# Attention with two heads per stack on the two row halves of TensorE, scores in a ring of three banks

## What is computed

```python
mod = silu(c) @ w_adaln + b_adaln                  # six shifts, scales and gates
h = modulate(ln(x), sh_msa, sc_msa)
q, k, v = heads(h @ w_qkv + b_qkv)                 # 16 heads, 18 channels each
attn = softmax(einsum('bhqd,bhkd->bhqk', q, k) * hd ** -0.5)
x = x + g_msa * (merge(einsum('bhqk,bhkd->bhqd', attn, v)) @ w_proj + b_proj)
xn = modulate(ln(x), sh_mlp, sc_mlp)
# top 2 of 4 experts: cw * (gelu(xn @ w1 + b1) @ w2 + b2), summed
return x + g_mlp * moe
```

## Time and profile before

| | |
|---|---|
| median of 3 runs | 991.68 us (991.67 to 992.36) |
| the profiled execution, its own time | 992.99 us |
| its span, first to last instruction | 991.2 us |
| TensorE busy | 900.9 us (91%), 5111 matmuls |
| TensorE weight loads | 639.9 us (65%) |
| VectorE, ScalarE, GpSimd busy | 566.0, 516.8, 313.3 us |
| DMA | 73.99 MB, mean 75 GB/s |
| scores and maxima on TensorE | 486 + 512 matmuls recorded, 212.4 and 167.7 us busy |
| exponentials on ScalarE, maxima on VectorE | 282.0 and 309.2 us |

### The profile page before, as it was taken

One profiled execution on the slowest core, in us unless ns is written; L12 is line 12 of the kernel. 1 busy time (PEld: TensorE's weight loads), 2 busy tenths in 40 slices (PEclk: granted clock), 3 DMA queues, 4 the chain that ended last, 5 costly groups with the idle time before them and its releaser, 6 DMA issues. The chain is left out here.

```text
span 991.2 us, 15201 instructions
## 1 busy us (share of the span) xinstructions
PE 900.9 (91%) x5111; PEld 639.9 (65%) x5111; DVE 566.0 (57%) x978; ACT 516.8 (52%) x1003; POOL 313.3 (32%) x314
## 2 busy tenths in 40 slices
PE   4878799999999999999999896438999999999995
PEld 3775444454545545555444375328999999999995
DVE  3767658767676776767774068463455444444342
ACT  1531266777776777777778735435443333333331
POOL 3522111012120111111042149626555444444342
PEclk9898799999999999999999969558999999999998
DMA  8051600624216060330631157405332222222221
GB/s 209 10 114 23 129 3 17 131 84 102 64 27 137 17 128 19 74 84 8 153 98 44 35 162 256 149 25 141 84 60 56 44 43 43 36 41 40 43 36 19
DMA packets 59296, 73.99 MB, mean 75 GB/s; under 512 B 24856, under 2 KB 51334, under 8 KB 58200
## 3 DMA queue, kind: packets, MB, share of 16 engines
q1 hardware_dynamic: 50216, 60.32, 24.5%
q0 software_dynamic: 8400, 12.12, 7.3%
q10 hardware_dynamic: 608, 0.59, 0.2%
HBM read 33.87 MB, written 15.73 MB: 50 GB/s over the span
## 5 line engine op out<-in xcount | busy, mean ns | idle before, releaser
L1014 DVE TENSOR_REDUCE negmax<-m_ps 128x1 f32<-128x1024 f32 x256 | 309.2, 1221 | 129.5 <-PE m_ps L1079 128.8
L1001 ACT ACTIVATE probs<-s_ps 128x512 f32<-128x512 f32 x486 | 282.0, 597 | 102.6 <-PE s_ps L1110 79.8
L1110 PE MATMUL s_ps<-stack 96*128 96x512 f32 x486 | 212.4, 444 | 5.4 <-ACT probs L1001 3.6
L1110 PEld LDWEIGHTS s_ps<-stack 96*128 96x128 f32 x486 | 90.7, 189 | 163.0 <-ACT probs L1001 130.3
L1079 PE MATMUL m_ps<-stack 96*128 96x512 f32 x512 | 167.7, 412 | 13.1 <-DVE negmax L1014 7.4
L449 POOL TENSOR_TENSOR parts<-proj_f,parts 128x512 fp32r<-128x512 f32 x32 | 41.0, 1282 | 322.0 <-ACT proj_f L443 322.0
L1124 PE MATMUL o_ps<-probs,v_aug 128*19 128x512 f32 x1024 | 136.1, 604 | 0.5 <-ACT probs L1001 0.5
L1969 PE MATMUL gate_bank<-weights,ht_hi 128*128 x630 | 127.1, 296 | 0.4 <-DVE ht_lo L1865 0.4
L1079 PEld LDWEIGHTS m_ps<-stack 96*128 96x128 f32 x512 | 97.9, 195 | 35.2 <-DVE negmax L1014 16.7
L1945 PE MATMUL h_ps<-weights,xt_hi 128*128 x525 | 115.7, 351 | 4.1 <-DVE xt_hi L1858 4.1
L1691 ACT CAST ht_hi<-ht_ps 128x384 fp32r<-128x384 f32 x105 | 43.5, 488 | 117.4 <-PE ht_ps L1956 117.4
(11 more groups left out here) (213 smaller groups left out, 1111.7 us busy)
## 6 DMA issues: line engine op xcount, KB each, us to landing
stack<-parts SPq DMA_DIRECT2D x96, 256.0 KB, 5.0
w_raw<-in_L_cond_w SPq DMA_DIRECT2D x9, 432.0 KB, 3.6
w_raw<-in_L_cond_w SPq DMA_DIRECT2D x9, 384.0 KB, 3.4
xn_scratch<-h SPq DMA_DIRECT2D x16, 192.0 KB, 3.7
x_in<-in_x SPq DMA_DIRECT2D x4, 576.0 KB, 9.6
o_scratch<-o_norm SPq DMA_DIRECT2D x16, 144.0 KB, 2.4
o_in<-o_scratch SPq DMA_DIRECT2D x16, 144.0 KB, 2.6
xr<-in_x SPq DMA_DIRECT2D x16, 144.0 KB, 3.1
```

The lines of the kernel that those rows point to most:

```text
L1001: nc.scalar.activation(probs[:, st % 2, h], score_bank(g, st, h), ACT.Exp, scale=SCALE)\
L1014: nc.vector.tensor_reduce(negmax[:, half, g % 2, m % 16:m % 16 + 1], m_ps[m % 2][:], AX.X, ALU.max, negate=True).then_inc(max_free, 1)
L1110: nc.tensor.matmul(score_bank(g, st, h), stack[s][:, h, 1, kt // QT, (kt % QT) * P:(kt % QT + 1) * P], stack[s][:, h, 0, half], start=True ...
```

## The change

- A stack now has 128 rows: two heads, each in a block of 64 rows (54 used for the three products of 18 rows, and two rows for the high and low part of the maximum; ones stand against these, written once by memsets on GpSimd). There are three stack buffers (`STACKS = 3`), and the stack of group g+2 is loaded in group g, by 12 transfers of 18 rows each.
- The maxima are matmuls of one head, 128 queries and 512 keys; a pair of two heads fills the two halves of a double bank, and one reduction gives two numbers. A second small reduction joins the two key halves. Scores are issued in pairs.
- `misc` is gone. Scores and projection units share a ring of three single banks (`s_ps`, `slot_mm`, `slot_free`), and rows and outputs take turns in the maxima's two double banks (`max_mm`, `max_free`). `MaxPlan` makes the list of turns: maxima run 12 steps ahead, rows are due at steps 4 and 12, outputs at 2 and 10; projection units stand at steps 2, 5, 9 and 12, each cut in two.
- ScalarE takes a projection out once; GpSimd makes the high part by a copy, and the low part.
- The last group no longer uses four banks.
- SyncE's loop has another order, and a row of maxima goes back by four transfers of one row instead of two.

The diff, cut to its core:

```diff
+    BLOCK = 64
+    MAX_ROW = 3 * HD
+    STACKS = 3
...
+    def ones_rows(self, pool, i):
+
+        for hh in range(2):
+            s = slice(hh * self.BLOCK + HP, (hh + 1) * self.BLOCK)
+            pool.memset(f32(self.stacks[i][s, :, 1]), 1.0).then_inc(self.ones_ok, 1)
+            pool.wait_ge(self.ones_ok, 2 * i + hh + 1)
...
-        sp.wait_ge(self.parts_ok, 4 * (g + 1))
-
-        n = HP
+        sp.wait_ge(self.parts_ok, self.parts_count(g, 3))
+        sp.wait_ge(self.ones_ok, 2 * min(g + 1, self.STACKS))
...
-                sp.dma_start(f32(self.stacks[g % 2][q * HP:q * HP + n, h]).rearrange("p a b n -> p a (b n)"),
-                             f32(self.parts[h * HP:h * HP + n, kind]).rearrange("p a b n -> p a (b n)"))\
+                row = (h % 2) * self.BLOCK + q * HD
+                sp.dma_start(f32(self.stacks[g % self.STACKS][row:row + HD, h // 2]).rearrange("p a b n -> p a (b n)"),
+                             f32(self.parts[h * HP:h * HP + HD, kind]).rearrange("p a b n -> p a (b n)"))\
...
+PAIR_BLOCKS = 2
+S_BANKS = 3
+AHEAD = 48
+RATE = 4
+PROJ_AT = (2, 5, 9, 12)
+UNITS = len(PROJ_AT)
+
+
+def score_item(g, st, h):
+
+    before = sum(GH * STEPS + UNITS * (i + 2 < GG) for i in range(g))
+    return UNITS + before + GH * st + h + sum(st > at for at in PROJ_AT if g + 2 < GG)
...
+        self.maxima(self.lead, BLOCKS)
+        self.turn(self.lead, "rows", 0)
+        self.maxima(self.lead, AHEAD)
+        due = []
+        for t, items in enumerate(self.steps):
+            g, st = t // STEPS, t % STEPS
+            begun = self.block // BLOCKS
+            self.maxima(items, AHEAD + RATE * t + 2)
+            for turn in due:
+                self.turn(items, "rows", turn)
+            if st == KT + 2:
+                self.turn(items, "out", 2 * g)
+            if st == 2 and g >= 1:
+                self.turn(items, "out", 2 * g - 1)
+            self.maxima(items, AHEAD + RATE * (t + 1))
+            due = range(begun, self.block // BLOCKS)
...
-                n, s = 2 * g + half, g % 2
-                sp.wait_ge(rows_step, 2 * (n + 1))
+                sp.wait_ge(max_free, 2 + plan.rows_at[2 * g + half] + 1)
                 for part, rows in enumerate((rows_hi, rows_lo)):
-                    sp.dma_start(rows_dram[g, half, part], f32(rows[:, half])).then_inc(rows_st[half], 16)
+                    sp.dma_start(rows_dram[g, half, part].rearrange("a b n -> (a b) n"), f32(rows[:, half]))\
+                      .then_inc(rows_st[half], 16)
                 sp.wait_ge(rows_st[half], 32 * (g + 1))
-                for part, q in enumerate((0, 2)):
-                    sp.dma_start(f32(stack[s][q * HP + HD:q * HP + HA, :, 0, half]),
-                                 rows_dram[g, half, part].rearrange("(a h t) n -> a h (t n)", a=1, h=GH))\
-                      .then_inc(rows_ld[half], 16)
+                for part in range(2):
+                    for hh in range(2):
+                        row = hh * heads.BLOCK + heads.MAX_ROW + part
+                        sp.dma_start(f32(stack[g % heads.STACKS][row:row + 1, :, 0, half]),
+                                     rows_dram[g, half, part, hh].rearrange("(a j t) n -> a j (t n)", a=1, j=PAIRS))\
+                          .then_inc(rows_ld[half], 16)
...
             load_rows_of_max(0, 0)
+            load_stack(1)
             for g in range(GG):
-                if g + 1 < GG:
-                    load_stack(g + 1)
-                if g == 0:
-                    load_rows_of_max(0, 1)
-                else:
-                    load_rows_of_max(g, 1)
+                load_w(g + 3)
+                if g >= 1:
                     store(g - 1, 1)
+                load_rows_of_max(g, 1)
+                if g + 2 < GG:
+                    load_stack(g + 2)
...
+                store(g, 0)
                 if g + 1 < GG:
                     load_rows_of_max(g + 1, 0)
-                store(g, 0)
                 if g == GG - 2:
                     for i in (2, 3):
                         late.load_piece(sp, 0, i)
-                load_w(g + 3)
...
+            def parts(g, u):
+                half, a = u // 2, u % 2
+                hi, lo = ((heads.Q_HI, heads.Q_LO), (heads.K_HI, heads.K_LO))[a]
+                pool.wait_ge(slot_free, S_BANKS + proj_item(g, u) + 1)
+                if u == 0:
+                    for h in range(GH):
+                        pool.wait_ge(stack_ld[h], 48 * g)
+                nc.gpsimd.tensor_copy(heads.parts[:, hi, half], heads.proj_f[:, u % 2]).then_inc(parts_ok, 1)
+                pool.wait_ge(parts_ok, heads.parts_count(g, u) - 1)
+                nc.gpsimd.tensor_tensor(heads.parts[:, lo, half], heads.proj_f[:, u % 2],
+                                        f32(heads.parts[:, hi, half]), ALU.subtract).then_inc(parts_ok, 1)
...
+                    if st == 0 and g >= 1:
+                        out_of_bank(2 * g - 1)
+                    if st == KT:
+                        out_of_bank(2 * g)
+                    if st in PROJ_AT and g + 2 < GG:
+                        project(g + 2, PROJ_AT.index(st))
...
+                nc.vector.tensor_reduce(negmax[:, half, first:first + count], m_ps[n % 2][:], AX.X, ALU.max, negate=True)\
+                  .then_inc(max_free, 1)
+                if first + count == BLOCKS:
+                    dve.wait_ge(max_free, 2 + n + 1)
+                    nc.vector.tensor_reduce(rowmax[:, half].rearrange("p (h b) -> p b h", h=2),
+                                            negmax[:, half].rearrange("p (b k h) -> p b h k", k=2, h=2), AX.X, ALU.min)\
+                      .then_inc(rowmax_ok, 1)
...
+                for i in range(count):
+                    if half == 0 and (first + i) % (BLOCKS // PAIRS) == 0:
+                        for hh in range(2):
+                            pe.wait_ge(stack_ld[2 * ((first + i) // (BLOCKS // PAIRS)) + hh], 48 * (g + 1))
+                    hh, kh, qt, j = ((first + i) % 2, (first + i) // 2 % 2, (first + i) // 4 % QT,
+                                     (first + i) // (4 * QT))
+                    r = slice(hh * heads.BLOCK, hh * heads.BLOCK + heads.MAX_ROW)
+                    mm = nc.tensor.matmul(m_ps[n % 2][:, i], stack[s][r, j, 0, half, qt * P:(qt + 1) * P], stack[s][r, j, 1, kh],
                                           start=True, stop=True)
...
+                for hh in range(2):
+                    k = score_item(g, st, 2 * j + hh)
+                    pe.wait_ge(slot_free, k + 1)
+                    r = slice(hh * heads.BLOCK, hh * heads.BLOCK + heads.MAX_ROW + 2)
+                    nc.tensor.matmul(s_ps[k % S_BANKS][:], stack[s][r, j, 1, kt // QT, (kt % QT) * P:(kt % QT + 1) * P],
+                                     stack[s][r, j, 0, half], start=True, stop=True).then_inc(slot_mm, 1)
...
+                for st in range(STEPS):
+                    items = plan.steps[STEPS * g + st]
+                    scores(g, st, 0)
+                    for it in items[:1]:
+                        item(*it)
                     if st >= 1:
                         values(g, st - 1)
                     elif g >= 1:
                         values(g - 1, STEPS - 1)
-                    scores(g, st, (2,))
-                    for tile in tiles[1:2]:
-                        maximum(*tile)
-                    scores(g, st, (3,))
-                    for tile in tiles[2:]:
-                        maximum(*tile)
-                    for turn in row_turns:
-                        rows(*turn)
-                    for turn in out_turns:
-                        outputs(*turn)
-                    for unit in units:
-                        project(*unit)
+                    scores(g, st, 1)
+                    for it in items[1:2]:
+                        item(*it)
+                    unit = PROJ_AT.index(st) if st in PROJ_AT and g + 2 < GG else None
+                    if unit is not None:
+                        project(g + 2, unit, slice(0, 4))
+                    for it in items[2:]:
+                        item(*it)
+                    if unit is not None:
+                        project(g + 2, unit, slice(4, len(PRODUCTS)))
```

More of the change, by code:

```diff
@@ L568, in _ @@
             nc.gpsimd.memset(f32(wqk_lo[:]), 0.0).then_inc(bias_zero, 1)
+            pool.wait_ge(bias_zero, 4)
+            for i in range(2):
+                heads.ones_rows(pool, i)
             def roots(b):
@@ new lines, with proj_item, __init__, maxima @@
+BLOCKS = 2 * GH * QT
+PAIR_BLOCKS = 2
[7 more added lines that the diff above has]
+    return UNITS + before + GH * st + h + sum(st > at for at in PROJ_AT if g + 2 < GG)
+def proj_item(g, u):
+    return u if g == 1 else score_item(g - 2, PROJ_AT[u], GH - 1) + 1
+class MaxPlan:
+    def __init__(self):
+        self.lead, self.steps, self.last = [], [[] for _ in range(STEPS * GG)], []
+        self.rows_at, self.out_at, self.count, self.block = {}, {}, 0, 0
+        self.maxima(self.lead, BLOCKS)
```

(44 more changed lines are left out.)

302 lines of the change are left out of this document (107 added, 195 removed).

## The result

The changed kernel takes 1088.1 us (median of 4 runs, 1085.9 to 1095.8) against 992.0 (991.7 to 993.6) for the kernel before on the same chips: a ratio of 1.098, 95% interval 1.092 to 1.104 (ratios leave out runs in a slower state of the chip, at a lower clock, of which there was one, the 965.6 of the first experiment). That is slower, as forecast, by 96 us where 51 were forecast, and above the range.

The account below looks back on a forecast made before the run. It took a loop within the step, not a full engine, to bound the kernel. Stage 410.0 + 10.2 + 46.8 + 45.9 = 512.9 against 459.8 (+53), -2 before the first score: 993.0 + 51 = 1044, median 1043, range 1010 to 1080.

Parts of the forecast that it names:

- SyncE's chain: SyncE's queue: next group's first score waits for rows of maxima behind twelve stack loads; 66.3 us for group 0.
- plain step: Attention loop with the third bank and overlapping pairs: 2.74 us a step, ends 2.66 and 2.97, against 3.30 before.
- step with a projection unit: Seven products between the maximum and next scores: values start 3.9 us after those before, 1.16 more a unit.
- stack load starts, after the group's first score: SyncE's load waits for the last projection unit at step 12; parts ready at 46.4 us of a 51.4 us group.
- late weights, groups 1 to 5: Transfers between stack loads and rows on SyncE: 5.0, 9.5, 3.5, 3.5 and 1.7 us, letting the queue drain.
- rows to DRAM and back, six times: Rows of maxima, first issue to the load's: 4.0 us behind a full queue in group 0, 1.8 in groups 1 to 5.
- six periods with their cold starts: Attention stage: 66.3 + 5 x 64.1 + 23.2 = 410.0 us, and 1.7 x 6 = 10.2 for a cold TensorE.
- groups 6 and 7: End of the attention stage: group 6 loads no stack, its rows in time, 46.8 us; group 7 45.9 us.
- I take 0.9: 10.8 in all, ends 7.4 and 13.8: Twelve stack loads of 18 rows: 0.9 us each, between 0.65 if bytes count and 1.15 if engines' rows count.
- Rival 3: Stack loads: transfers of 18 rows no shorter than of 32, 1.15 us each, 18 in all: 1061; chance 0.20.
- the first (rows in time, 931): SyncE does not hold the rows of maxima back, each group takes its 51.4 us: total 931; chance 0.13.
- The second (no overlap): TensorE's pairs on two row halves don't run side by side: +21 us, 1064; chance 0.13.

Follow-up runs that it names:

- the first experiment: Changed kernel with SyncE's store and the rows of maxima of the next group issued ahead of the stack load: 954.9 us (951.1 to 965.6), ratio 0.962.
- its queue is put right: Changed kernel with the store and rows of maxima ahead of the stack loads, and the late weights ahead of both: 949.1 us, ratio 0.956.
- the repaired queue: For the row-half comparison: changed kernel with only the store and rows of maxima moved ahead of the stack loads, 954.9 us; on one row half 1019.1.

## Why the prediction was wrong

The direction, the cause and its place were right. What failed are the sizes, most of them in SyncE's chain and nearly all too small, and their sum is outside the range. By the prediction's own steps, with after's profile against it:

| step | forecast | measured |
|---|---|---|
| plain step | 2.74 | 2.83 |
| step with a projection unit | 3.9 | 4.13 (198.54 to 202.67) |
| stack load starts, after the group's first score | 46.4 and 1.7 cold | 46.9, 49.0, 49.1, 49.0, 49.1, 50.3 |
| twelve loads, six times | 64.8 | 81.1 |
| late weights, groups 1 to 5 | 23.2 | 33.1 |
| rows to DRAM and back, six times | 13.0 | 17.3 |
| landing | 1.9 | 1.3 to 1.5 |
| six periods with their cold starts | 420.2 | 452.8 |
| groups 6 and 7 | 92.7 | 103.5 |
| stage | 512.9 | 556.3 |
| ahead of the first score | -2 | +1.0 (110.07 for 109.09) |
| behind the last store | 0 | -4.7 (417.6 for 422.3), not explained |

**The step that failed first** is "I take 0.9: 10.8 in all, ends 7.4 and 13.8". It measured 1.13 and 13.5, near the upper end, 16.3 us of the 43 by which the stage is longer than forecast. Rival 3, which said so, had a chance of 0.20, and the prediction gave its reason away: "two rows remain on the busiest engine". The nine engines are there (share 0.54), but the load of 16 rows shows that it is not their count that sets the time. I split the difference between two mechanisms, where the only row at hand timed transfers of the same 8 KB rows, and its price should have been kept. The lower end of 7.4 was out of reach in any case, since an issue of 18 rows took SyncE 0.8 us with nothing queued: 9.4 or more for twelve.

**The second** is the late weights, priced at 23.2 from the earlier trace rows, where they stood behind other work and met a queue with room. Behind twelve loads they took 33.1. Of the difference 2.4 stood in the trace of before: from the times of one group the prediction took 3.5, 3.5 and 1.7 for groups 3 to 5, which took 5.2, 3.9 and 2.0 there. The other 7.5 came with the new place. The prediction said in the same sentence that they "let the queue drain (1.8 for 4.0, so 64.1)"; it counted what they gave the rows and not what the full queue cost them. The rows' chain was not relieved by all of it either: 17.3 for 13.0 (3.95, 3.77 and 3.00 in the first three groups, 2.2 in the others).

**The third** is the last two groups, 103.5 for 92.7: I charged a cold start to each of the six periods, the last of which ends at group 6's first score, so that its cost falls into group 6. And I charged 1.7 us, from a wait of 2.85 us. After 18.67 us of idle, TensorE kept the lower clock for 16.4 us; values stood 4.47 us apart in place of 2.83:

```profile
564.00 1.91 PE L1179 MATMUL o_ps<-probs,v_aug 128*19 128x512 f32 x8
568.47 1.91 PE L1179 MATMUL o_ps<-probs,v_aug 128*19 128x512 f32 x8
```

Two such steps, and a third of 5.39 that holds the transposes of outputs (3.34 at the upper clock), are 5.3 of the 10.8 us; the rest I have not taken apart. How long the clock would stay low was chance for a forecast: the first four cold starts lasted about a quarter of the last.

Of the rivals, the first (rows in time, 931) is what the kernel does once its queue is put right, at 949: its bookkeeping of 51.4 for a group measured 53.0. The second (no overlap) was wrong, and would have cost more than the 21 us it was given: in the repaired queue the kernel on one row half is 64 us slower.

## What to carry to other kernels

When a program loads ahead, look at what stands behind the load in the same queue and is needed sooner. Here the load and the late weights cost 139 us, because the first score of the next group waited for what stood behind them; a step that is 0.47 shorter, 128 times, is worth 60. Price a transfer by its kind and by what is in the queue ahead of it, and when two mechanisms give two prices, put the range around both rather than a value between them. A buffer ring should be tested alone: here the pairs without the third bank would have left the step at its old length.

## What the hardware showed that was not expected

- Twelve transfers within SBUF with rows of 8 KB were issued in 12.90, 13.5 and 13.76 us for 16, 18 and 32 rows, about 6.5 GB/s a row. With 17 rows, all on one engine, they took 44.97, and by the rate of 27 GB/s a transfer took some 5.2 us: one row fewer made it about four times as long.
- An issue says nothing of the end of the data: the DMA engines worked for some 4 us behind the last of twelve issues of 18 rows.
- The same wait does not cost the same clock. After 24.0 us of idle the granted clock was back at full speed in 4.0 us, after 18.7 us only in 16.4, in both cases with TensorE busy without a pause until then. Waits of 8.3 to 22.6 us in the other kernels show the same scatter (8.3 us: 13.3; 22.6 us: 16.3; 11.3 us: 3.7 in one case and 13.3 in another). In the kernel on one row half it stayed at 0.50 for 30 us in which TensorE was busy all the time. What makes the difference was not tried.
